# Third stage of a graph and attention kernel: one edge tile in each step from the sixth on, in place of five in four steps

## What is computed

```python
xn = layernorm(x)
# two graph convolutions over the same edges (dst is sorted)
h   = tanh(mean_over_edges(xn[src] -> dst) @ W1_l.T + xn @ W1_r.T + b1)
gnn =      mean_over_edges( h[src] -> dst) @ W2_l.T +  h @ W2_r.T + b2
# linear attention over all nodes
q, k, v = split(xn @ w_qkv);  q_phi, k_phi = elu(q @ proj) + 1, elu(k @ proj) + 1
mix = (q_phi @ (k_phi.T @ v)) * (1 / (q_phi @ k_phi.sum())) @ w_proj + b_proj
x = x + gnn + mix
# top-1 mixture of 8 experts
x = x + gate * expert(layernorm(x))
```

## Time and profile before

| | us |
|---|---|
| median of 3 runs | 2736.06 |
| lowest and highest | 2735.32, 2736.74 |
| the profiled execution | 2733.61 |
| its span, first to last instruction | 2731.8 |
| mean granted clock of TensorE | 0.984 |

### The profile page before, as it was taken

The page is one execution under the profiler, slowest core; times in us unless marked ns, Lnnn a source line. Parts: engine busy times, 40 slices in busy tenths (PEclk is TensorE's granted clock), DMA queues, the critical chain, the costliest instruction groups (busy, mean ns, idle before and its releaser), DMA issues.

```text
span 2731.8 us, 36032 instructions
## 1 busy us (share of the span) xinstructions
PE 2612.9 (96%) x11712; PEld 2081.5 (76%) x11712; DVE 1836.8 (67%) x3708; ACT 1031.0 (38%) x1805; POOL 1061.6 (39%) x1009
## 2 busy tenths in 40 slices
PE   5999999999999989999999788999999899999999
PEld 4788888888888868888886556677777677777777
DVE  5577777777778744444443677788886677777774
ACT  3455454444444434443443232233332132232232
POOL 5677766666666620000000455555554111111110
PEclk9999999999999999999999899999999999999999
DMA  9767665555555554444444478787887332232231
GB/s 367 246 174 201 174 194 145 146 139 135 145 125 157 126 156 180 189 172 185 185 185 162 147 192 224 217 241 220 233 227 179 145 139 93 94 137 93 105 125 46
DMA packets 134566, 460.66 MB, mean 169 GB/s; under 512 B 26649, under 2 KB 27161, under 8 KB 99137
## 3 DMA queue, kind: packets, MB, share of 16 engines
q1 hardware_dynamic: 98624, 375.21, 37.6%
q0 software_dynamic: 35840, 84.23, 17.0%
HBM read 240.62 MB, written 218.76 MB: 168 GB/s over the span
## 4 chain that ended last, share of the span: by engine, by line
PE 82%; DMA 7%; DVE 5%; SPq 2%; issue 2%; ACT 2%; POOL 1%; POOLq 0%; DVEq 0%; ACTq 0%
PE bank L1206 63%; PE bank L1257 8%; DMA agg_d<-O,eidx 5%; PE bank L1213 3%; PE bank L1321 2%; DVE x2T_low L314 2%; PE bank L1421 1%; PE bank L417 1%; PE bank L418 1%; SPq L484 1%; DVE f_relu L1125 1%; PE bank L1332 1%; ACT f_relu L884 1%; SPq L486 1%; PE bank L1406 1%
## 5 line engine op out<-in xcount | busy, mean ns | idle before, releaser
L378 POOL DMA_INDIRECT agg_d<-O,eidx x160 | 275.4, 1721 | 234.6 <-DMA agg_d<-O,eidx 165.7
L314 POOL TENSOR_TENSOR G_low<-G,G_high 128x512 fp32r<-128x512 f32 x160 | 244.0, 1525 | 209.0 <-ACT G_high L439 209.0
L361 POOL DMA_INDIRECT G<-y_d,esrc x80 | 87.2, 1090 | 529.8 <-DMA y_d<-b_y 516.9
L397 DVE SCALAR_TENSOR_TENSOR Sj<-erow,dstf,tri 128x128 f32<-128x128 int32 x160 | 188.7, 1179 | 55.4 <-DMA agg_d<-O,eidx 55.3
L720 POOL TENSOR_SCALAR veps<-mv 128x1 f32<-128x1 f32 x80 | 26.5, 332 | 487.2 <-DVE mv L1098 487.2
L439 ACT CAST G_high<-G 128x512 fp32r<-128x512 f32 x160 | 99.2, 620 | 198.5 <-DVE G L958 175.4
L406 DVE SCALAR_TENSOR_TENSOR eidx<-cnt,todump,dstf 128x1 int32<-128x1 f32 x160 | 139.7, 873 | 7.6
L685 POOL TENSOR_TENSOR pd<-pd,low 128x512 f32<-128x512 f32 (+1 forms) x80 | 143.2, 1790 | 0.0
L314 POOL TENSOR_TENSOR a_xn_rows_low<-a_x,a_xn_rows_high 128x512 fp32r<-128x512 f32 x80 | 142.7, 1783 | 0.2 <-ACT a_xn_rows_high L749 0.2
L850 ACT CAST qz_high<-low 128x512 fp32r<-128x512 f32 x80 | 49.6, 620 | 239.4 <-PE bank L1206 152.5
L1206 PE MATMUL bank<-Wk_high,xnT_high 128*128 128x512 f32 x320 | 127.9, 400 | 6.3 <-DVE xnT_low L314 6.3
(11 more groups left out here) (201 smaller groups left out, 7981.8 us busy)
## 6 DMA issues: line engine op xcount, KB each, us to landing
agg_d<-zero SPq DMA_DIRECT2D x20, 1040.0 KB, 20.1
b_agg<-agg_d SPq DMA_DIRECT2D x20, 1040.0 KB, 8.8
a_x<-in_x SPq DMA_DIRECT2D x20, 1024.0 KB, 7.1
agg_d<-z_halves SPq DMA_DIRECT2D x20, 1024.0 KB, 5.9
q_d<-q_rows SPq DMA_DIRECT2D x80, 256.0 KB, 2.4
r_d<-r_rows SPq DMA_DIRECT2D x80, 256.0 KB, 3.8
r_in<-r_d SPq DMA_DIRECT2D x20, 1024.0 KB, 6.8
hT_d<-low SPq DMA_DIRECT2D x20, 1024.0 KB, 4.9
```

Of the source, the lines that this page charges most:

```text
L314: return eng.tensor_tensor(out_, full, high.bitcast(F32), ALU.subtract)
L361: pool.indirect_dma_start(G[:, j, :], None, table, bass.IndirectOffsetOnAxis(ap=esrc[:, b, j:j + 1], axis=0)).then_inc(e_g[j], 16)
L378: pool.indirect_dma_start(agg, bass.IndirectOffsetOnAxis(ap=eidx[:, j, 0:1], axis=0), O[:, j, 0:width], None, compute_op=ALU.add).then_inc ...
L397: dve.scalar_tensor_tensor(Sj[:, :], row, dstf[:, b, j:j + 1], tri[:, :], ALU.is_equal, ALU.mult, accum_out=cnt[:, j:j + 1]).then_inc(e_cn ...
```

## The change

The table now gives one edge count to each step from t = 6 on. Before, the steps t = 11, 15, 19, 23, 27 and 31 had two, so that at t = 32 the edge count had caught up with the step (s = t). Now s = t - 6 everywhere, `ahead` is -6 and no longer 0, and each engine that works on edges runs `mix` up to step 90: POOL and ACT up to 85 before, DVE up to 88, PE up to 87. The last scatter (tile 79, s = 83) moves from step 83 to step 89, the last edge sum (s = 82) from step 82 to step 88. The number of instructions of each kind stays.

```diff
         for t in range(32):
-            now = 0 if t < 6 else 1 + (t >= 8 and t % 4 == 3)
+            now = 0 if t < 6 else 1
             mix_edges.append([(s // 8, s % 8) for s in range(done, done + now)])
             done += now
         ahead = done - 32
...
-            turns(pool, mix, 6, head=4, last=1)
+            turns(pool, mix, 11, head=4, last=1)
...
-            turns(act, mix, 6, head=4, last=1, skip=5)
+            turns(act, mix, 11, head=4, last=1, skip=5)
...
-            turns(dve, mix, 9, head=4, last=1)
+            turns(dve, mix, 11, head=4, last=1)
...
-            turns(pe, mix, 8, head=4, last=1, skip=6)
+            turns(pe, mix, 11, head=4, last=1, skip=6)
```

## The result

The changed kernel takes **2723.62 us** (median of 20 runs, 2711.86 to 2734.85), the kernel before 2736.28 us beside it (20 runs, 2728.19 to 2741.74). The ratio is 0.9957 (95% interval 0.9945 to 0.9968): 12.7 us less, where 14 were forecast. The profiled execution took 2718.32 us, with a span of 2716.5.

The account below looks back on a forecast made before the run. A chain of scatters was taken to bound steps up to 31, PE the later ones. The fourth stage starts 15.6 us earlier, less 1.6 charged: 14 us off 2733.6 gives 2719.6 profiled, 2722 as median; range 2711 to 2738.

Parts of the forecast that it names:

- The two bounds: Third stage: one scatter in flight at a time bounds steps up to 31 (7.20 us a gap), PE later (7.13 a step).
- PE's largest gain: Third stage: PE reaches step 80 at 2037.2 instead of 2084.78, 47.6 us earlier, without reaching the stage's end.
- first rival: End of third stage: the chain holds PE's pace, so PE's gain reaches the end; 30 us less, 2706; chance 0.08.
- the chain would end last: End of third stage: last scatter issued at 2103, landed at 2107.7; PE's pause grows from 7.8 to some 33 us.
- the rival of the slow chain: Third stage: scatters beside denser loads keep long landings, 7.37 us a gap; stage ends 7 us later, 2743; chance 0.15.
- The tail: Scatters of tiles 70 to 79: 55 us taken, between 50.8 and 56.9, against 56.92 before.
- From the landing to the fourth stage: Last scatter's landing to DVE's start of the fourth stage: 9.8 us, between 8.8 and 11.2, with five 1 MB transfers.
- The charge of 1.6 us for line 624: Start of fourth stage: line 624's load waits for a store and comes late for DVE; 1.6 us, ends 0 and 5.
- The clock: PE at the fourth stage's start: its clock already falls in the short pause, so the longer one adds nothing.
- The chain no faster than now: Third stage: tile 70 stays at 2052.44 and the tail at 56.92 us; gain 7.6 us, 2728; chance 0.22.
- The loads between the stages: Before the fourth stage: five transfers at once make line 618 or 624 late by 5 to 8 us; 2728; chance 0.10.
- The rule on the landing: Scatter of 256 KB: the skill page's fit gives 2.6 us, the trace 4.7 alone and 6.8 in the early median.

Follow-up runs that it names:

- the first profile: Profiled execution of the changed kernel, nothing altered, on the first chip: 2718.32 us.
- the second profile: Profiled execution of the changed kernel, unaltered, on another chip: 2724.24 us; median of its runs 2722.99 us, ratio 0.9948.
- the pads spread: Changed kernel with POOL's clearing of pads spread over steps 10 to 14 instead of all in step 10: 2722.65 us, ratio 0.9939.
- the busy PE: Changed kernel with 52 products on constants added on PE after the last scatter landed, ahead of the fourth stage: 2723.63 us, ratio 0.994.
- the kernel before with a short scatter: Kernel before, third stage's scatter writing 128 of 512 columns to a buffer of its own: 2711.71 us, ratio 0.9909.
- the short scatter: Changed kernel, third stage's scatter writing 128 of 512 columns to a buffer of its own: 2702.61 us, ratio 0.9881.
- less load: Changed kernel with the third stage's x and q tiles loaded by 256 columns only, 128 KB for 1 MB: 2711.54 us, ratio 0.991.

## Why the prediction was right

**The two bounds** were read rightly: the chain of scatters in the steps before 32, PE later. PE's largest gain was given as 47.6 us and is 46.4 relative. What the prediction doesn't set apart is how much of it the six later steps take, chain or no chain: 35.8 us, so that 10.7 are left at the last edge sum. The forecast goes by the last scatter and isn't touched by this, and its first rival has the six steps in its sum. The bank, the second limit of the double steps, isn't in the prediction; the change takes it away too, and it enters no term.

**Where the gain goes.** The step that the chain would end last and leave PE waiting some 33 us held: 30.24 us. In the first profile tile 27 is at 1744.16 (1745.8 forecast), tile 70 at 2049.37 (2048) and the last scatter at 2101.71 (2103); but its stage began 3.1 us later, so relative to it the chain was faster than forecast, and in the second profile it was slower: tile 70 at 536.3 relative, where 526.1 was forecast. The mean gap is 7.11 in one and 7.28 in the other. The forecast, 7.09, stands at the lower edge. The lag of 12.2 us that tile 27 was to have behind step 37 is 5.9 in the first profile (1744.16 - 1738.27): the chain was nearly level with PE. The denser load on the DMA engines in 1525 to 1746 us (224 GB/s in place of 193) is what the rival of the slow chain named, and the gaps of 7.24 to 7.30 in five of the runs are near the point of 7.30 from which the gain was to be gone. It isn't gone there, because the tail and the terms behind it were charged too high.

**The tail** from tile 70 on is the term that pays for it: 55 us were taken, 51.4 to 52.3 are measured in the changed kernel, with the pads spread and with the busy PE. The lower end, 50.8, was nearer than the value I took: in the first profile eight of the nine gaps are 5.37 to 5.74 us, and only the one behind tile 71 (7.72) stands beside a load of x. The two errors, up to 10 us in the middle and 3 in the tail, have opposite signs.

**From the landing to the fourth stage** 9.8 us were taken, and 8.8 and 9.2 measured in the two profiles, though five transfers stand there: line 618 landed in 8.18 and 8.59 us. The charge of 1.6 us for line 624 was for nothing; the fifth `pre` came 12.1 us after the first, as before.

**The clock** is the term that was wrong: "I add nothing". The clock falls to 0.58 where it was 0.74 to 0.77, and the two rows at the start of the fourth stage cost 2.4 us more in the first profile of the changed kernel and 1.3 in the second. That this comes of the longer pause isn't shown: the kernel before with a short scatter pays 2.4 us behind a pause of 7.86. By luck it stands against 1.6 us and some 1 us that were charged too much elsewhere.

**The rivals.** PE's gain reaching the end was what happened with the short scatter, at about the price given; the landing of the full one excludes it. The chain no faster than now describes the second profile, whose last scatter is at 587.9 against 587.5 relative: its execution is 9.4 us shorter than that of the profile before, where this rival gave 7.6. The spread of the single runs (2712 to 2735) is as wide as the distance between the forecast and its rivals, so the median falls near 2722 partly by luck. The loads between the stages cost nothing where they stood, and 8.6 us where they were moved ahead of the last scatters.

**The rule on the landing.** The last scatter landed in 4.70 us, and rows of 4.5 to 4.9 us are the shortest in the chains of all runs with a scatter of full length. The estimate of 2.6 us for such a DMA that stood in the prediction, worked out from the Trainium skill, DMA: Bandwidth & Descriptors, in the section on the anatomy of one DMA, is not seen in any of them. The section names no kind of DMA for its fit, and no figure of it is for an accumulating scatter.

**What stays open.** Why a chain with the same work in front of it has gaps of 7.11 us in one execution and 7.28 in the next wasn't settled. With less load the spread of the runs shrinks to 2 us (four runs), which points to the loads that stand beside a scatter; which of them, and when, was not separated.

## What to carry to other kernels

Where two limits stand close to each other, taking the first away is worth the distance to the second: work out when the second would end, from the same trace, before the first is priced. A serial chain of transfers has to be costed by its own gaps, in the stretches where it alone was the limit, and with the loads that will stand beside it after the change. And transfers that were issued early to be ready in time were paid for, in both kernels tried here, by the transfer that is waited for.

## What the runs showed of the hardware

- An indirect accumulating scatter of 256 KB landed in 4.5 to 4.9 us with little beside it, in 5.88 and 6.92 beside a load of 1 MB, in 8.97 beside two, and in 11.01 beside four transfers. With a quarter of the bytes the last scatter landed in 3.25 us against 4.70, and the shortest gap between two of them is 4.0 us against 5.28: most of such a scatter's time isn't its bytes.
- Fifty-two products on constants brought PE's granted clock to 1.00, and after a pause of 2.91 us the transposes were at 0.55: work ahead of a sparse start didn't carry over.
- A second edge sum in a bank that has just been used waited 1.81 us for the copy; a second bank took the wait away (a double step of 10.32 us in place of 12.35) and no time.
